# Gathers of the second attention issued one at a time

## The reference

```python
x = x + L0_xattn(layernorm(x), ctx, ctx, mask)      # first attention
x = x + L0_ffn(layernorm(x))                        # 2 shared experts, 2 of 8 routed ones per token
x = x + L1_xattn(layernorm(x), ctx, ctx, padding)   # second attention
x = x + L1_ffn(layernorm(x))                        # sqrt((x cos W)^2 + (x sin W)^2)

# in L0_ffn, for each token:
gpk, i_topk = top_k(sigmoid(u @ centroids), 2)
h_r = (gk[..., None] * routed_all[i_topk]).sum(axis=-2)   # two weighted rows of 256
```

## Time and profile before

| | |
|---|---|
| median of 3 runs | 1362.75 us (1359.85 to 1372.66) |
| profiled execution, span from first to last instruction | 1366.7 us |
| TensorE busy | 1299.0 us, 95% of the span |
| ScalarE busy | 1036.6 us, 76% |
| VectorE busy | 739.8 us, 54% |
| GpSimd busy | 178.9 us, 13% |
| mean granted TensorE clock | 0.967 |

### The profile page before, as it was taken

One profiled execution on the slowest core, in us unless ns is written; L12 is line 12 of the kernel. 1 busy time (PEld: TensorE's weight loads), 2 busy tenths in 40 slices (PEclk: granted clock), 3 DMA queues, 4 the chain that ended last, 5 costly groups with the idle time before them and its releaser, 6 DMA issues. The chain is left out here.

```text
span 1366.7 us, 27234 instructions
## 1 busy us (share of the span) xinstructions
PE 1299.0 (95%) x9750; PEld 613.3 (45%) x9750; DVE 739.8 (54%) x1622; ACT 1036.6 (76%) x1482; POOL 178.9 (13%) x220
## 2 busy tenths in 40 slices
PE   8999999999999999978999999879989999999995
PEld 5422332333333566547999989532223323323322
DVE  5246686576575765235666666624514544433336
ACT  3699999999999745232666666347979999999993
POOL 4111120110020200630000000343210000000000
PEclk9999999999999999999999999977999999999997
DMA  8566745534536050411343343544120010010001
GB/s 225 132 213 219 220 124 156 165 124 157 185 121 228 17 185 1 143 47 40 96 140 114 114 132 107 137 131 102 53 60 1 32 51 1 31 51 1 1 1 61
DMA packets 105888, 140.78 MB, mean 103 GB/s; under 512 B 24915, under 2 KB 77522, under 8 KB 105790
## 3 DMA queue, kind: packets, MB, share of 16 engines
q1 hardware_dynamic: 88368, 102.13, 24.8%
q0 software_dynamic: 9888, 29.76, 6.9%
q10 hardware_dynamic: 7534, 7.57, 1.9%
HBM read 77.11 MB, written 51.69 MB: 94 GB/s over the span
## 5 line engine op out<-in xcount | busy, mean ns | idle before, releaser
L829 ACT ACTIVATE prob<-banks 128x1024 f32<-128x1024 f32 (+1 forms) x832 | 770.7, 1067 | 53.4 <-PE banks L1546 37.7
L1560 PE MATMUL banks<-prob,v 128*32 128x512 f32 (+1 forms) x3328 | 451.3, 615 | 1.1 <-ACT prob L829 1.1
L1546 PE MATMUL banks<-zone,kst 52*128 52x512 f32 (+1 forms) x1664 | 339.3, 472 | 15.8 <-ACT prob L829 11.0
L1546 PEld LDWEIGHTS banks<-zone,kst 52*128 52x128 f32 (+1 forms) x1664 | 138.9, 182 | 362.3 <-ACT prob L829 319.1
L2160 PE MATMUL banks<-xsT_d,w 128*128 128x128 f16 x1776 | 125.5, 221 | 3.4 <-issue 2.9
L1560 PEld LDWEIGHTS banks<-prob,v 128*32 128x32 f32 (+1 forms) x3328 | 65.9, 108 | 131.7 <-issue 109.1
L2160 PEld LDWEIGHTS banks<-xsT_d,w 128*128 128x128 f16 x1776 | 110.4, 99 | 13.0 <-issue 9.4
L2171 PE MATMUL banks<-w,hh 128*128 128x256 f16 x592 | 107.5, 274 | 0.0
L1070 DVE RECIPROCAL late<-late 128x512 f32<-128x512 f32 x31 | 103.9, 3353 | 1.1
L1967 DVE TENSOR_TENSOR hl<-hid,hh 128x128 f16<-128x128 f32 x296 | 83.3, 292 | 33.6 <-ACT hh L1898 25.9
L1065 DVE COPY late<-banks 128x512 f32<-128x512 f32 x31 | 21.4, 690 | 145.2 <-PE banks L1560 126.8
(11 more groups left out here) (270 smaller groups left out, 1267.7 us busy)
## 6 DMA issues: line engine op xcount, KB each, us to landing
weight_parts<-late SPq DMA_DIRECT2D x54, 256.0 KB, 3.4
w<-weight_parts POOLq DMA_DIRECT2D x24, 512.0 KB, 3.8
zone<-q_parts SPq DMA_DIRECT2D x180, 64.0 KB
late<-in_L_ffn_W_r SPq DMA_DIRECT2D x43, 256.0 KB, 4.0
kst<-kparts SPq DMA_DIRECT2D x88, 100.1 KB
q_parts<-qparts SPq DMA_DIRECT2D x16, 512.0 KB, 2.8
weight_parts<-more SPq DMA_DIRECT2D x26, 256.0 KB, 3.2
slot_rows<-late POOLq DMA_DIRECT2D x14, 384.0 KB, 3.9
```

The lines of the kernel that those rows point to most:

```text
L829: nc.scalar.activation(prob[0:m, t % P_RING, 2 * (n % 2):2 * (n % 2) + 2, :], score[G % S_RING][0:m, :, :], ACT.Exp, scale=0.25 / WSCALE). ...
L1546: last = nc.tensor.matmul(score[G % S_RING][0:m, a, :], kst[stack, 2 * q + n % 2, t * P:t * P + m].bitcast(F32R), qst[stack, u % Q_RING, n ...
L1560: last = nc.tensor.matmul(outp[u % 2][GROUP * j:GROUP * (j + 1), :], v[0:m, t, u % NQ, j, :], prob[0:m, (u * KT + t) % P_RING, j, :], star ...
```

## The change

A function `gather_in_turn` takes the place of the loop over the eight gathers for chunks 1, 2 and 3. Before each gather but the first of a chunk GpSimd waits until those issued so far have landed. The gathers of chunk 0 are left as they are, and so are the consumers.

```diff
+            def gather_in_turn(c):
+                for n in range(GATHERS):
+                    if n:
+                        pool.wait_ge(gathered[c], 16 * n)
+                    gather(pool, back, c, n, gathered[c])
+
...
             if not first:
                 pool.wait_ge(v_ready, KT)
-                for n in range(GATHERS):
-                    gather(pool, back, 1, n, gathered[1])
+                gather_in_turn(1)
             pool.wait_ge(bo_loaded, 16)
             add_bias(0)
             for c in range(NC):
...
                 if not first and 2 <= c + 2 < NC:
                     pool.wait_ge(added, GATHERS * (c + 2))
-                    for n in range(GATHERS):
-                        gather(pool, back, c + 2, n, gathered[c + 2])
+                    gather_in_turn(c + 2)
```

## The result

The changed kernel takes 1368.97 us (median of 20 runs, 1360.81 to 1378.99) against 1362.12 us for the kernel before in the same session (20 runs, 1351.26 to 1372.66). The ratio is 1.0057, 95% interval 1.0031 to 1.0083: 0.6% slower, 7 to 8 us. Forecast were +3.7 us and 1367, with "within 1%" as the likeliest; the time is inside the range. The two spans, 1366.7 and 1367.8, differ by only 1.1, because the work ahead of the first gather of chunk 1 took 9.2 us less in the profile after (899.68 against 908.93). So the two traces are compared from that gather on.

What follows compares the result with a forecast made beforehand. TensorE, busy 95% of the span, was taken as the bound. The gate 8.8 us later less 5.1 given back made +3.7: 1370.4 against the profiled 1366.7, 1366.5 as a median, given as 1367; range from 1356 less 1 to 1378 plus 1.

Steps and rivals of the forecast that it cites:

- Chunk 1's landing: Chunk 1's eight chained gathers: seven periods of 3.5 us plus 3.74 for the last, 28.2 us in all.
- From chunk 1's sum to chunk 2's first gather: Sum, moments, root, normalisation and GpSimd's bias, all in line: 13.0 us, as in the profile before.
- Chunk 2's landing: Chunk 2's eight chained gathers, where only gathers run: seven periods of 3.05 us plus 2.8, 24.2 us.
- From there to the gate: VectorE's sum and moments of chunk 2, two halves of the query split, then TensorE: 7.3 us.
- The gate: TensorE's first output product of unit 2, held by VectorE's query split: opens 8.8 us later, TensorE idling some 12 us.
- Gate to the copy of unit 2: Without the third burst's freeze this stretch takes 26.5 us in place of 31.6, giving 5.1 us back.
- Costed at nothing: Chunk 3's late arrival, the store and loads of chunk 1's queries, and `scales(0)` behind chunk 3's gathers: 0 us.
- Sum: Whole kernel: 8.8 us later at the gate less 5.1 us given back, +3.7 us.
- Rival A: ScalarE's freezes stay because the bursts do not make them; +8.8 us, 1371.6 us; chance 0.18.
- B: Landing is the long part: 4.03 us per gather, 31.9 per chunk; +15.2 us, 1378 us; chance 0.15.
- C: Gathers at the scatters' period of 2.67 us, 21.0 per chunk; -6.8 us, 1356 us; chance 0.12.
- the dearest rival: The case of long landings in chunks 1 and 2, both taking 31.9 us: +15.2 us; chance 0.15.

Runs made afterwards that it cites:

- e5_keys_held: Changed kernel with SyncE's last 24 key loads held until chunk 1 has landed; ratio 1.0156 against the kernel before.
- e4_stats_later: Changed kernel with VectorE's sum and moments of chunk 2 moved behind the query splits of chunk 1; ratio 1.0077 against the kernel before.
- e1_third: Kernel before with only chunk 3's gathers one at a time, chunks 1 and 2 in bursts; ratio 1.0001 against the kernel before.
- e8_third_quiet: Kernel before with chunk 3's burst held until unit 3 has begun; ratio 0.9990 against the kernel before.
- a_again: The changed kernel, unchanged, run again in the third session; 1359.24 us, ratio 1.0192 against the kernel before.
- e3_second: Kernel before with only chunk 2's gathers one at a time, chunks 1 and 3 in bursts; ratio 1.0034 against the kernel before.
- e6_best: Changed kernel with chunk 1 back in a burst and VectorE's sum and moments of chunk 2 after chunk 1's query splits; ratio 0.9981 against the kernel before.
- b_third: The kernel before, unchanged, run again in the fourth session, which freezes; ratio 1.0020 against the kernel before.
- e9_best_again: The kernel of e6_best, unchanged, run again in the fourth session, which freezes; 1339.1 us, ratio 0.9885 against the kernel before.

## Why the prediction was right, and where it was off

The forecast of a small loss, within 1%, held, and most terms of the sum did, counted from the first gather of chunk 1:

- **Chunk 1's landing: 28.2 forecast, 34.2 measured.** This is the term that was mis-sized. I took 3.5 us per gather because "its neighbours stay". They did not: before, the last gather was issued at 917.95, ahead of SyncE's 24 key loads (from 920.87 on); stretched to 34 us, the gathers run into them, and three periods grew to 7.3, 6.6 and 4.3. A chain that is stretched meets other company. e5_keys_held gives 6.0 of it back. The mean period of chunk 1 was 4.5, outside the 2.7 to 4.0 that the prediction itself set as its limit; that of chunk 2 was 3.0.
- From chunk 1's sum to chunk 2's first gather: 13.0 forecast, 13.1 measured (933.86 to 947.00).
- Chunk 2's landing: 24.2 forecast, 23.9 measured, in the quiet stretch.
- From there to the gate: 7.3 forecast, 7.2 measured (970.88 to 978.11).
- The gate: 8.8 later forecast, 14.5 measured (78.4 after the first gather against 64.0). TensorE idled 12.0, "some 12" as forecast, but by luck: the gate opened 5.7 later than forecast, and TensorE, held up 13.0 at the first turn, came there 6.4 later (66.5 after the first gather, against 60). e4_stats_later showed that the wait at the gate goes away with another order on VectorE.
- Gate to the copy of unit 2: 26.5 forecast, 26.3 measured, so 5.3 given back.
- Costed at nothing and so it was: chunk 3's late arrival (e1_third, no change), the query store and loads, `scales(0)` (from the copy of unit 3 to the end 339.1 before and 339.6 after).
- Sum: +3.7 forecast, 14.5 - 5.3 = +9.2 measured in the stretch, 7 to 8 in the runs. The miss is the 6.0 of chunk 1's landing.

Rival A (the freezes stay) fell: no freeze with one gather in flight or two, in any profile, and they follow a burst that is moved. The Trainium skill ("DMA: Bandwidth & Descriptors", Queues, rings and completion order) says that each DMA engine takes its queues in turn, packet by packet; by that rule a burst could not hold up another queue's transfer so long. No run here tests the rule: in e8_third_quiet there was no other queue's transfer to hold up, and ScalarE froze all the same. What it lacked then is open. Of B, the landing was the long part for one chunk, not for both: 34 and 24 against 31.9 for each. C fell: with no other load beside it, the period was 3.0, of which 2.0 to 2.1 is idle waiting after the 0.94 of the issue; beside other loads it was up to 9.5 (a_again). The estimate of 2.7 that the prediction took from the Trainium skill ("DMA: Bandwidth & Descriptors", Anatomy of one DMA — SWDGE (gpsimd) path) was the same case, and too low by 0.3 even there.

What the prediction missed as a whole: it took the freezes for a fixed part of the kernel before. They come and go with the session. Its +3.7 and the measured +7 to +8 hold where the kernel freezes; where it does not, the same change costs 1.9%, 25.7 us, more than the +15.2 of the dearest rival. That the comparison was made in a session with freezes was luck.

## What to carry to other kernels

Spacing transfers out costs their landing time once per transfer, and that counts if the last of them stands on the path; a depth of two hid most of it and kept the benefit. Ask what a stretched transfer will now run beside. And where an engine waits in program order for rows that it does not need yet, move that wait behind the work that others wait for: here the order alone took 14.7 us from the changed kernel's stretch of 104.8 (e4_stats_later). Giving chunk 1 its burst back took 20.6 (e3_second, which has chunk 3's too; that one is worth nothing by e1_third), and both together 28.1 (e6_best). Against the kernel before, that last version was 0.2% faster where nothing freezes and 1.2% faster where the bursts freeze. Last, compare inside one session, and look in its profile for what the change is meant to remove.

## What the runs showed of the hardware that was not expected

- Eight indirect transfers issued 1.26 us apart froze ScalarE for 2 to 6 us per burst, beginning 5 to 9 us after the first issue, in two sessions of four. It did so in each of the ten bursts of chunks 1 to 3 profiled there (three each in the kernel before, b_third and e8_third_quiet, one in e9_best_again). One in flight (five chunks in those two sessions) or two (three chunks) never did. In the other two sessions none of the ten bursts of chunks 1 to 3 did. Chunk 0's burst, which stands in every kernel, shows nothing either way: ScalarE has few instructions then, and its longest idle time beside the burst is 4.6 to 5.1 us in both kinds of session.
- In the sessions that freeze, the expert stage loses time too, while its scatters run two at a time: ScalarE's idle times at the GELU sum to 59.1, 51.8, 45.6, 50.3, 48.9 and 51.5 us in six profiles, against 42.6 in all eight of the other two sessions. I made no experiment on these, so whether the scatters cause them is open, as is what differs between the sessions. It isn't the chip alone, if its number means the same device: the third session, without freezes, and the fourth, with them, are both recorded on chip 2. The same kernel took 1333 us in two of the sessions, 1354 and 1362 in the others, and its runs spread over 4 to 6 us in the first two and over 21 us in each of the others.
- The granted clock fell during the 12 us wait at the gate and was back at the higher level some 6 us after the restart at 978.11, against 4 us after 999.38 before. Stretches of the changed kernel (columns as in the earlier trace rows):

```profile
981.00:984.00 3.00, 3.00 (x14) 0.70 (x12) 2.93 (x3) 1.93 (x3) 0.00 (x0) 0.50 0.00 0
984.00:986.00 2.00, 2.00 (x13) 0.41 (x11) 0.33 (x1) 1.76 (x2) 0.00 (x0) 0.87 0.04 8
```
